# Spreading dt by DMA from DRAM in a selective scan, with two vector operations on GpSimd

## The reference, cut to what matters

```python
x_dbl = einsum('bld,rd->blr', xs, x_proj_w)
dt = softplus(einsum('blr,dr->bld', x_dbl[..., :8], dt_proj_w) + dt_proj_b)
Bm, Cm = x_dbl[..., 8:24], x_dbl[..., 24:]
A = -exp(A_log)
def step(h, inp):                       # h: (b, d, n)
    xt, dtt, Bt, Ct = inp
    h = exp(dtt[..., None] * A) * h + dtt[..., None] * Bt[:, None, :] * xt[..., None]
    return h, einsum('bdn,bn->bd', h, Ct)
```

## Time and profile before

| | |
|---|---|
| median of 3 runs | 6361.38 us (6359.47 to 6361.48) |
| the profiled execution, its own time | 6361.27 us |
| its span | 6359.3 us |
| layer 1, first to last scan begun | 4013.7 to 6344.1 us |
| busy share of the span: PE, DVE, ACT, POOL | 92%, 79%, 59%, 66% |
| DMA queue 1: share of 16 engines' span, bytes moved | 9.4%, 169.73 MB |

### The profile page before, as it was taken

One profiled execution on the slowest core, in us unless ns is written; L12 is line 12 of the kernel. 1 busy time (PEld: TensorE's weight loads), 2 busy tenths in 40 slices (PEclk: granted clock), 3 DMA queues, 4 the chain that ended last, 5 costly groups with the idle time before them and its releaser, 6 DMA issues. The chain is left out here.

```text
span 6359.3 us, 93797 instructions
## 1 busy us (share of the span) xinstructions
PE 5868.1 (92%) x28212; PEld 2757.3 (43%) x28212; DVE 5011.0 (79%) x7254; ACT 3777.6 (59%) x7359; POOL 4188.6 (66%) x3147
## 2 busy tenths in 40 slices
PE   7999999999999999999999997888888888888887
PEld 3444444444444444444444442333333333333333
DVE  7777777777777777777777773798999998899988
ACT  3666566656666666666666665655556655556655
POOL 2677766776666776666677764566666666666666
PEclk9999999999999999999999998898989998889988
DMA  4011011011011011011000001000000000000000
GB/s 128 22 38 41 26 32 41 25 41 42 26 32 36 29 42 39 27 32 31 14 21 22 9 17 41 15 22 16 15 15 17 15 21 15 15 15 17 15 21 11
DMA packets 143428, 175.15 MB, mean 28 GB/s; under 512 B 64832, under 2 KB 88256, under 8 KB 141504
## 3 DMA queue, kind: packets, MB, share of 16 engines
q1 hardware_dynamic: 142944, 169.73, 9.4%
HBM read 109.11 MB, written 58.98 MB: 26 GB/s over the span
## 5 line engine op out<-in xcount | busy, mean ns | idle before, releaser
L560 POOL TENSOR_TENSOR sums<-exps 128x512 f32<-128x512 f32 x2048 | 2620.2, 1302 | 1309.9 <-ACT exps L493 1305.2
L569 DVE TENSOR_REDUCE mpart<-ps 128x1 f32<-128x512 f32 x4096 | 2539.8, 682 | 820.7 <-PE ps L369 820.7
L493 ACT ACTIVATE exps<-ps 128x512 f32<-128x512 f32 x4096 | 2127.8, 602 | 1404.5 <-PE ps L376 1404.1
L1218 POOL TENSOR_TENSOR hc<-hh,c_rep 128x512 f32<-128x512 f32 x1024 | 1490.0, 1458 | 825.8 <-DVE hh L1189 824.9
L369 PE MATMUL ps<-k_st,q_ring 96*128 96x512 f32 x4096 | 1753.7, 429 | 19.0 <-DMA k_st<-qk_split 9.4
L376 PE MATMUL ps<-q_ring,k_st 98*128 98x512 f32 x4096 | 1621.0, 397 | 4.0 <-ACT exps L493 3.6
L1189 DVE TENSOR_TENSOR_SCAN hh<-d_a,carry,ps 128x512 f32<-128x512 f32 x1024 | 1297.6, 1270 | 2.1
L369 PEld LDWEIGHTS ps<-k_st,q_ring 96*128 96x128 f32 x4096 | 774.7, 189 | 1065.6 <-DVE mpart L569 529.4
L1103 ACT ACTIVATE d_a<-ps,a_neg 128x512 f32<-128x512 f32 x1027 | 706.6, 688 | 726.3 <-PE ps L988 688.3
L387 PE MATMUL ps<-exps,v_ring 128*32 128x512 f32 x8192 | 1090.8, 605 | 0.0
L988 PE MATMUL ps<-s_dt,sel_g 128*128 128x512 f32 x1028 | 638.6, 621 | 324.0 <-ACT d_a L1103 319.7
(11 more groups left out here) (110 smaller groups left out, 3409.0 us busy)
## 6 DMA issues: line engine op xcount, KB each, us to landing
qk_split<-hilo SPq DMA_DIRECT2D x128, 256.0 KB, 2.3
q_ring<-qk_split SPq DMA_DIRECT2D x384, 64.0 KB, 2.0
k_st<-qk_split SPq DMA_DIRECT2D x45, 512.0 KB, 7.2
za<-z_ext SPq DMA_DIRECT2D x33, 320.0 KB, 3.1
zp<-z_ext SPq DMA_DIRECT2D x33, 320.0 KB, 4.0
xc<-in_x SPq DMA_DIRECT2D x32, 256.0 KB, 3.0
v_dram<-v_stage SPq DMA_DIRECT2D x32, 256.0 KB, 2.3
v_ring<-v_dram SPq DMA_DIRECT2D x16, 512.0 KB, 3.8
```

The costliest lines, as they stand in the source:

```text
L493: nc.scalar.activation(exps[:, u % 4, CH * half:CH * half + CH], a_bank(("exp", n, t)), ACT.Exp, scale=SCALE).then_inc(a_done, 1)
L560: pool.tensor_tensor(sums[:, u % 8, :], exps[:, u % 4, 0:CH], exps[:, u % 4, CH:2 * CH], ALU.add).then_inc(summed, 1)
L569: nc.vector.tensor_reduce(mpart[:, m % 2, t % 4, t // 4:t // 4 + 1], d_bank(("max", m, t)), AX.X, ALU.max).then_inc(d_done, 1)
L1218: pool.tensor_tensor(hc[:, g % NHC, :], hh[:, g % NHH, :], c_rep[:, p, :], ALU.mult).then_inc(hc_ready, 1)
```

## The change

dt is no longer spread by PE. POOL adds the two parts of softplus at g = 20 and multiplies by xs at g = 21, in place of DVE. SP stores the sum (128 x 2 x 512) to a DRAM tensor `dt_dram`, and loads it back 32 times a chunk, each time 8 rows of 2 KB, every row to 16 partitions, straight into a buffer of the ring `d_a`. ACT's `decay` works in place on that buffer. The stack `s_dt`, its two `high` and two `low` pieces and `repeat_dt` are gone. The free PSUM bank goes to the u ring (NU = 4), `d_a` has 16 buffers, and SP's program is written out instead of looped. `high` and `low` for u move to g = 25 and 26.

```diff
+    dt_dram = nc.dram_tensor("dt_dram", [2, INNER, LC], F32, kind="Internal").ap()
-        DT_BANK, U_BANK, Y_BANK, O_BANK, ITEM_BANK = 0, 1, 4, 5, 6
-        NU = 3
+        U_BANK, Y_BANK, O_BANK, ITEM_BANK = 0, 4, 5, 6
+        NU = 4
-        s_dt = sb("s_dt", [128, 2, 4, LC], F32R)
-        NDA, NHH, NHC = 8, 8, 8
+        NDA, NHH, NHC = 16, 8, 8
+        dt_in = [sem(f"dt_in{i}") for i in range(NDA)]
+        def channels(g):
+            half, jj, i = g // 16, g // 4 % 4, g % 4
+            return 128 * half + 32 * i + GC * jj
 # SP
+                def store_dt(j, p):
+                    sp.wait_ge(dt_sum, j + 1)
+                    sp.dma_start(dt_dram[p].rearrange("(h q) l -> q h l", h=2), dt[:, :, :]).then_inc(dt_stored, 16)
+                def load_dt(j, p, g):
+                    if g == 0:
+                        sp.wait_ge(dt_stored, j * 16 + 16)
+                    c = channels(g)
+                    sp.dma_start(d_a[:, g % NDA, :], dt_dram[p, c:c + GC, :].rearrange("c (o l) -> c o l", o=1).to_broadcast([GC, ST, LC])
+                                 ).then_inc(dt_in[g % NDA], 16)
+                def emit(it, p):
+                    for t in range(G):
+                        if t == G - NDA:
+                            store_dt(it + 1, 1 - p)
+                        sp.wait_ge(scanned, it * G + t + 1)
+                        if t + NDA < G:
+                            load_dt(it, p, t + NDA)
+                        else:
+                            load_dt(it + 1, 1 - p, t + NDA - G)
+                        if t == 18 and it:
+                            store(it - 1, 1 - p)
+                        if t == 26 and it + 2 <= NIT:
+                            load(it + 2, p)
 # PE
-                def repeat_dt(it, p, g):
-                    ...
-                    ge(pe, scanned, u_bank_free(it, g))
+                    ge(pe, scanned, it * G + g - NU + 1)
 # ACT
-                            ge(act, lo_ready, j * 4)
+                            ge(act, u_prod, j)
+                            ge(act, dt_stored, j * 16)
-                        high(j, p, s_dt, dt, g - 25)
-                    elif g in (27, 28):
                         act.wait_ge(u_prod, j + 1)
-                        high(j, p, s_u, ux, g - 27)
+                        high(j, p, s_u, ux, g - 25)
-                    act.wait_ge(dt_rep, it * G + g + 1)
-                    ge(act, scanned, it * G + g - NDA + 1)
-                    nc.scalar.activation(d_a[:, g % NDA, :], ps[:, DT_BANK, :], ACT.Exp,
+                    act.wait_ge(dt_in[g % NDA], it * (16 * G // NDA) + 16 * (g // NDA) + 16)
+                    nc.scalar.activation(d_a[:, g % NDA, :], d_a[:, g % NDA, :], ACT.Exp,
 # DVE
-                    if g == 20:
-                        nc.vector.tensor_tensor(dt[:, :, :], dt[:, :, :], edt[:, :, :], ALU.add).then_inc(dt_sum, 1)
-                    elif g == 21:
-                        nc.vector.tensor_tensor(ux[:, :, :], dt[:, :, :], xs[:, p, :, :], ALU.mult).then_inc(u_prod, 1)
-                    elif g in (25, 26):
-                        low(j, p, s_dt, dt, g - 25, 0)
-                    elif g in (27, 28):
-                        low(j, p, s_u, ux, g - 27, 1)
+                    if g in (25, 26):
+                        low(j, p, s_u, ux, g - 25)
 # POOL, behind the hc of the same group
+                def prepare(j, p, g):
+                    if g == 20:
+                        pool.wait_ge(sp_log, j * 2 + 2)
+                        pool.tensor_tensor(dt[:, :, :], dt[:, :, :], edt[:, :, :], ALU.add).then_inc(dt_sum, 1)
+                    elif g == 21:
+                        pool.wait_ge(dt_sum, j + 1)
+                        pool.tensor_tensor(ux[:, :, :], dt[:, :, :], xs[:, p, :, :], ALU.mult).then_inc(u_prod, 1)
```

More of the change, by code:

```diff
@@ L814, in layer1 @@
         (z_in, flipped, item, item_read, sp_log, dt_sum, u_prod, hi_ready, lo_ready,
-         dt_rep, u_rep, da_ready, bu_ready, scanned, kept, hc_ready, y_done, y_added, gated, z_used, o_ready, o_copied,
-         o_full, o_even, o_odd) = [sem(x) for x in (
+         u_rep, da_ready, bu_ready, scanned, kept, hc_ready, y_done, y_added, gated, z_used, o_ready, o_copied,
+         o_full, o_even, o_odd, dt_stored) = [sem(x) for x in (
              "z_in", "flipped", "item", "item_read", "sp_log", "dt_sum", "u_prod",
-             "hi_ready", "lo_ready", "dt_rep", "u_rep", "da_ready", "bu_ready", "scanned", "kept", "hc_ready", "y_done",
-             "y_added", "gated", "z_used", "o_ready", "o_copied", "o_full", "o_even", "o_odd")]
+             "hi_ready", "lo_ready", "u_rep", "da_ready", "bu_ready", "scanned", "kept", "hc_ready", "y_done",
+             "y_added", "gated", "z_used", "o_ready", "o_copied", "o_full", "o_even", "o_odd", "dt_stored")]
+        dt_in = [sem(f"dt_in{i}") for i in range(NDA)]
         XS, XD, DT, BI, CI, GATE, GI, NITEM = 0, 2, 3, 5, 6, 7, 9, 10
         G = GROUPS
-        LEAD = 4
         def ge(e, s, value):
@@ L835, in column @@
             return 2 * half + i // 2, jj + 4 * (i % 2)
-        def u_bank_free(it, g):
-            before = g - NU if g >= NU else max(k for k in range(G) if k % NU == g % NU) - G
-            return it * G + before + 1
+        def channels(g):
+            half, jj, i = g // 16, g // 4 % 4, g % 4
+            return 128 * half + 32 * i + GC * jj
         def steps(e, prepare, emit, tail):
@@ L856, in load @@
                 def load(j, p):
-                    jw = j if isinstance(j, int) else j % NIT
+                    jw = j % NIT
                     b, lc = jw // STEPS, jw % STEPS
@@ L873, in store @@
                     sp.dma_start(out[b, :, bass.ds(lc * LC, LC)], o_sb[:, p, :]).then_inc((o_even, o_odd)[p], 16)
+                def store_dt(j, p):
[20 more added lines that the diff above has]
+                            load(it + 2, p)
                 load(0, 0)
                 load(1, 1)
[L877 to L883, removed]
+                store_dt(0, 0)
+                for g in range(NDA):
+                    load_dt(0, 0, g)
+                for it in range(NIT):
+                    emit(it, it % 2)
                 store(NIT - 1, 1)
@@ L887, in _ @@
                 sp.wait_ge(o_odd, 16 * (NIT // 2))
+                for i in range(NDA):
+                    sp.wait_ge(dt_in[i], 16 * (NIT * G // NDA + 1))
                 sp.wait_ge(z_in, 64 * (NIT + 1))
@@ L992, in repeat_u @@
                     if g == 0:
-                        pe.wait_ge(lo_ready, it * 4 + 4)
-                    ge(pe, scanned, u_bank_free(it, g))
+                        pe.wait_ge(lo_ready, it * 2 + 2)
+                    ge(pe, scanned, it * G + g - NU + 1)
                     nc.tensor.matmul(ps[:, U_BANK + g % NU, :], sel_g[:, j, :], s_u[:, p, s, :], start=True, stop=True).then_inc(u_rep, 1)
@@ L1000, in emit @@
                     for g in range(G):
-                        if isinstance(it, int) and it == g == 0:
-                            for d in range(LEAD):
-                                repeat_dt(it, p, d)
                         repeat_u(it, p, g)
@@ L1016, in emit @@
                             sum_states(it, g // 4 - 2)
[L1017 to L1020, removed]
                 def tail():
@@ L1076, in prepare @@
                     elif g in (25, 26):
-                        act.wait_ge(dt_sum, j + 1)
-                        high(j, p, s_dt, dt, g - 25)
-                    elif g in (27, 28):
                         act.wait_ge(u_prod, j + 1)
-                        high(j, p, s_u, ux, g - 27)
+                        high(j, p, s_u, ux, g - 25)
                     elif g == 29:
@@ L1124, in tail @@
                 def tail():
-                    for g in range(LEAD - 1):
-                        decay(NIT, g)
                     for g in range(G - KEEP, G):
@@ L1135, in _, with low @@
             def _(dve):
-                def low(j, p, stack, src, part, n):
+                def low(j, p, stack, src, part):
                     a, b = slice(64 * part, 64 * part + 64), slice(64 - 64 * part, 128 - 64 * part)
-                    dve.wait_ge(hi_ready, j * 4 + 2 * n + part + 1)
+                    dve.wait_ge(hi_ready, j * 2 + part + 1)
                     nc.vector.tensor_tensor(stack[b, p, part::2, :], src[a, :, :], stack[a, p, part::2, :].bitcast(F32), ALU.subtract
@@ L1143, in prepare @@
                 def prepare(j, p, g):
-                    if g == 20:
-                        dve.wait_ge(sp_log, j * 2 + 2)
-                        nc.vector.tensor_tensor(dt[:, :, :], dt[:, :, :], edt[:, :, :], ALU.add).then_inc(dt_sum, 1)
-                    elif g == 21:
-                        dve.wait_ge(dt_sum, j + 1)
-                        nc.vector.tensor_tensor(ux[:, :, :], dt[:, :, :], xs[:, p, :, :], ALU.mult).then_inc(u_prod, 1)
-                    elif g in (25, 26):
-                        low(j, p, s_dt, dt, g - 25, 0)
```

(7 more changed lines are left out.)

## The result

The changed kernel takes 6252.61 us (median of 4 runs, 6242.23 to 6261.45), the kernel before 6360.43 (now 4 runs, one more than above): the ratio is 0.983, with a 95% interval of 0.9813 to 0.9847. It is faster, by 108 us, where 339 were forecast, and 6252.6 lies outside the range of 5970 to 6135. The profiled execution has a span of 6251.0 us.

What follows compares the result with a forecast made beforehand. DVE was taken to set the pace: 60.8 us of work plus 1.5 of waits, 62.3 us a chunk against 72.9, so 339 us less over 32 chunks, 6022 us from 6361.3. The 8-in-10 range was 5970 to 6135.

Steps and rivals of the forecast that it cites:

- its chunk without waits: DVE's work per chunk if it never waits: 65.8 us before, 60.8 after, so 5.0 us leave.
- The two POOL operations: Sum and product moved from DVE to POOL: 2.5 us each, bounds 4.6 and, for both, 2.4.
- The chain behind scan 20: POOL's list from scan 20's end: sum at 3.8, product at 7.6 us; ACT's `high` in time for DVE by 0.9.
- 1.76 us if 8 engines carry it: Time of one dt load if only 8 DMA engines carry it; the chunk would then take 62.0 us.
- the rivals: PE keeps DVE waiting, 0.12; POOL late, 6102 us, 0.12; loads serial, 6998 us, 0.06; another engine holds the pace, 0.02.
- the first rival: PE keeps DVE waiting as today because the low clock lasts longer: as far as 6201 us, chance 0.12.
- the part on the DMA path: Loads 28.2 us plus z, output and dt store make 34 of 60.8 us a chunk: hidden.
- The slack of a ring of 16: In the dt load buffers, later loads have 16 groups, 28 us, ahead of them.
- the 1.5 us a chunk: DVE's waits left after the change: 1.5 us a chunk, bounds 0 and today's 7.1.
- the short pauses: Part of DVE's 7.1 us of waits a chunk before the change, beside 6.3 for PE's spread of u.
- The lead of two groups: With NU = 4, PE's spread of u gets 3.5 us of lead instead of 1.8, covering 2.2 us lost at low clock.
- The edit to GpSimd: Sum and product leave DVE for POOL, 1.12 us each off DVE's chunk; delays cost no more than tenths.

Runs made afterwards that it cites:

- z_early_unroll: z_early with the programs of PE, ACT, DVE and POOL written out for all 32 chunks instead of looped: 5990.33 us, ratio 0.9419.
- k16: The changed kernel with a group's partitions ordered (state, channel), so a dt load has 16 copies outermost, not 8 channels: 6100.91 us, ratio 0.9584.
- z_early: The changed kernel with z loads out of the burst, za and stage_j issued at t = 8, zp a chunk later at t = 2: 6063.12 us, ratio 0.9529.
- z_early_k16_unroll: z_early_unroll with the (state, channel) partition order of k16 added: 5989.96 us, ratio 0.9416.

## Why the prediction was wrong

**What held.** DVE sets the pace, and its chunk without waits is 60.8 us: z_early_unroll, with almost no waits left, runs at 61.4. The two POOL operations were given 2.5 us each and took 2.36. The chain behind scan 20 was right to 0.3 us: the store of dt goes out at 3.8, the product ends at 7.3 (7.6 in the text). The dt loads are hidden for `decay`, 3.1 us of waits in the whole layer. Of a load I said 1.76 us if 8 engines carry it; k16 bears the 8 out, and with 205 GB/s in the burst a load takes about 256 KB / 205 GB/s = 1.3 us. So none of the rivals came about by the mechanism that I gave it, though the first one's sign did: DVE waits for PE's spread as much as before.

**What failed** is the part on the DMA path, at the words "3.6 + 0.7 + 1.4 for z, output and dt store, 34 of 60.8: hidden". It adds engine time over a chunk and asks only when `decay` needs a dt load. It does not ask what stands behind the dt loads in SP's list. The change puts the z loads, which had a loop of their own, at t = 26, behind the wait for the sum at t = 16 and eleven loads, and PE needs them at g = 1 of the next chunk. In the kernel before PE reached them 14 us after their first issue at 5531.69, and they had landed; after, the last is issued 8.7 us behind the first, and lands when PE has waited 9 us. Their place in the chunk hardly moved (1.0 and 2.6 us behind scan 26). What ate the slack is the issue that lasts 7 us, and a PE that comes 6.8 us sooner, which the change was made for. The slack of a ring of 16 was counted for the dt loads; z had only the end of a chunk, and I gave it no line of its own.

In numbers: 6252.6 - 6022 = 231 us of error. z_early takes away 189 of them and lands at 6063, inside the range. Of its 41 us above the forecast 22 are pauses of DVE (2.2 us a chunk at the spread and at the jumps, where I had left 1.5) and 11 the slower `low`; the rest I can't place. Written-out programs take 73 more, to 5990. This lies 32 us under the forecast, because of the 1.5 us a chunk only some 0.6 were then needed. The jumps were in the kernel before too, 43 us there, and I took the 0.95 us of DVE's idle time in them as part of the short pauses; that DVE stands idle four times as long at each (3.7 us) in the changed kernel I did not see.

**The clock.** I named the low clock as the first rival. The granted clock is 0.90 in the chunk shown (0.91 before); PE idles and is granted the low clock, but in z_early that costs DVE at most 18.2 us in the whole layer. In z_early_unroll the clock is 0.91, as before the change, and DVE waits 12.7 us for PE. The lead of two groups covers it, as forecast.

**The edit to GpSimd** was booked as a gain of 2 x 1.12 us a chunk, with its delay inside the 1.5 us. In the changed kernel it is a loss of 66 us, in the kernel before of 98, and a gain of 30.5 only in z_early. The 2.6 us by which it makes the sum late sit on the path to the z loads, and nearly every us there counts.

## What to carry to other kernels

When a queue gets new transfers, write down its list in order and ask of each entry behind them, old ones above all, who needs it and when; a DMA share of 0.44 says nothing about an entry that stands behind a wait and its backlog. Put transfers with distant needs ahead of the wait, not behind. An operation moved to a slower engine is a gain only if nothing on the path hangs on its end: the same move changed the time by +98, +66 and -30.5 us in three settings of this kernel. And the outermost dimension of a small broadcast load decides how many DMA engines carry it.

## What was unexpected in the hardware

- The issue of one z transfer on SP took 7.04 us behind a burst of eleven loads on 8 engines, 1.72 us where 16 engines carried them, and 0.43 us (median) where no burst stood ahead of it (z_early). So it seems that transfers not yet carried away hold the issuing engine, and with it all later entries of its list.
- A jump back of the two-chunk loops costs the kernel before 3.1 us, and z_early, with its loads at 160 GB/s, 5.2 us; 16 engines instead of 8 for the same bytes gave 2.1 us of it back at each jump (30 / 14). The Trainium skill (Runtime: NRT & Kernel Launch, Instruction fetch mechanics) says that a taken branch out of the prefetched code waits for a DMA fetch of its target. The idle times at the jumps fit this, 3.7 us of DVE for nothing that the profile shows against 0.95 in the kernel before, and so does their end in the written-out programs; no view shows the fetch itself. That it is slow because it shares DMA engines with the loads fits these runs but was not shown by itself.
- `hc` on POOL slows from 1.27 to 2.3 us beside a two-input DVE instruction in SBUF. It seems to work the other way too: in z_early a `low` on DVE took 1392 ns on the mean, with the sums off POOL 1220.
- The same bytes took more engine time on 16 engines than on 8: at 164 GB/s in both the DMA share was 0.60 in z_early_k16_unroll and 0.48 in z_early_unroll (window 4100 to 4700), and the kernels were equally fast.
